# The tower's two state products moved behind the column-tile products, with new places for every step

## What is computed

```python
Z = jnp.einsum('bhsd,bhse->bhsde', v, k)          # k, v after a causal convolution
gl = Z.reshape(Bx, H, Sx, HD * HD) @ gk + gb
gates = (jax.nn.relu(gl) ** 2 + EPS)[..., None]
attn = jnp.cumsum(gates * Z, axis=2) / (jnp.cumsum(gates, axis=2) + EPS)
o = jnp.einsum('bhsd,bhsde->bhse', q, attn)
o = o / jnp.maximum(jnp.linalg.norm(o, axis=3, keepdims=True), EPS)
```

## Time and profile before

| | |
|---|---|
| Median of 3 runs | 1988.42 us (1988.13 to 1988.78) |
| The profiled execution | 1988.27 us, span from first to last instruction 1986.1 us |
| TensorE, TensorE weight loads | busy 1850.2 us (93%), 1588.0 us (80%) |
| VectorE, ScalarE, GpSimd | busy 1165.6 us (59%), 733.4 us (37%), 439.4 us (22%) |
| Granted TensorE clock, mean | 0.982 of full |

### The profile page before, as it was taken

How to read it: one execution, slowest core, us unless ns; L and a number is a source line. 1 busy time by engine, 2 the same in 40 slices (tenths; PEclk the granted TensorE clock), 3 DMA queues, 4 the chain that set the end, 5 groups by cost and what they waited for, 6 DMA issues and landing times.

```text
span 1986.1 us, 41766 instructions
## 1 busy us (share of the span) xinstructions
PE 1850.2 (93%) x17146; PEld 1588.0 (80%) x17146; DVE 1165.6 (59%) x3019; ACT 733.4 (37%) x1444; POOL 439.4 (22%) x391
## 2 busy tenths in 40 slices
PE   4799999999999999969899999999999999999998
PEld 3678888888888888758688888888888888888887
DVE  2668888888888888755554344434444444444443
ACT  1334444554455555334323322232233223322332
POOL 3233223333222222111121122112211221122112
PEclk8899999999999999989899999999999999999999
DMA  3000000000000000022000000000000000000000
GB/s 94 5 12 18 18 17 18 16 19 16 18 17 16 15 5 9 18 86 80 17 22 1 22 22 22 1 22 22 22 1 22 22 22 1 22 22 22 1 22 22
DMA packets 29211, 42.38 MB, mean 21 GB/s; under 512 B 5856, under 2 KB 22624, under 8 KB 29024
## 3 DMA queue, kind: packets, MB, share of 16 engines
q1 hardware_dynamic: 23648, 33.49, 5.1%
q0 software_dynamic: 2048, 4.20, 0.8%
q10 hardware_dynamic: 3328, 2.04, 0.4%
HBM read 22.93 MB, written 16.78 MB: 20 GB/s over the span
## 4 chain that ended last, share of the span: by engine, by line
PE 73%; DVE 17%; issue 4%; DMA 3%; POOL 2%; ACT 1%; SPq 1%; another core or an unknown queue 0%; DVEq 0%; POOLq 0%; ACTq 0%
PE ps L1406 11%; PE ps L1407 10%; PE ps L1408 10%; PE ps L806 3%; PE ps L1008 3%; PE ps L1456 3%; PE ps L1472 3%; DVE bxn L1271 3%; PE ps L887 3%; PE ps L807 3%; PE ps L808 3%; PE ps L959 3%; PE ps L937 2%; DVE bstats L1255 2%; DMA h<-h_rows 2%
## 5 line engine op out<-in xcount | busy, mean ns | idle before, releaser
L1245 POOL TENSOR_TENSOR hids_low<-hid,hids_high 128x512 fp32r<-128x512 f32 x96 | 137.6, 1440 | 611.0 <-ACT hids_high L1392 611.0
L512 POOL TENSOR_TENSOR rstd<-var,minus_half 128x4 f32<-128x4 f32 x80 | 82.5, 1032 | 564.5 <-DVE var L599 564.4
L757 ACT ACTIVATE xn<-x,shift,rstd 128x128 f32<-128x128 f32 x320 | 130.3, 482 | 133.6 <-DVE shift L604 133.6
L676 DVE TENSOR_TENSOR att<-ps,causal 128x512 f32<-128x512 f32 x256 | 158.6, 681 | 18.1 <-PE ps L937 18.0
L1406 PE MATMUL ps<-r_high,wq_high 128*128 128x256 f32 x512 | 147.4, 288 | 0.7 <-issue 0.7
L1407 PE MATMUL ps<-r_low,wq_high 128*128 128x256 f32 x512 | 144.9, 283 | 0.0
L1408 PE MATMUL ps<-r_high,wq_low 128*128 128x256 f32 x512 | 144.8, 283 | 0.0
L1386 ACT ACTIVATE silu<-ps 128x512 f32<-128x512 f32 x96 | 57.4, 598 | 226.5 <-DVE hid L1321 159.9
L1008 PE MATMUL ps<-w_f,wide 128*128 128x128 f32 x1024 | 130.1, 278 | 0.2 <-ACT wide L801 0.2
L1008 PEld LDWEIGHTS ps<-w_f,wide 128*128 128x128 f32 x1024 | 120.8, 192 | 6.0 <-issue 5.0
L1308 DVE TENSOR_TENSOR m_low<-ps,m_high 128x512 fp32r<-128x512 f32 x32 | 22.1, 692 | 170.8 <-ACT m_high L1378 170.8
(11 more groups left out here) (352 smaller groups left out, 5060.9 us busy)
## 6 DMA issues: line engine op xcount, KB each, us to landing
h_rows<-h_out SPq DMA_DIRECT2D x16, 512.0 KB, 2.8
h<-h_rows SPq DMA_DIRECT2D x16, 512.0 KB, 3.8
out<-bxn SPq DMA_DIRECT2D x32, 256.0 KB, 2.6
taps<-in_filters ACTq DMA_DIRECT2D x1, 1024.0 KB
emb<-in_embed,idx POOLq DMA_INDIRECT x64
wk<-in_W_kT SPq DMA_DIRECT2D x1, 1024.0 KB, 6.6
stage<-in_W_vT SPq DMA_DIRECT2D x2, 512.0 KB, 6.6
stage<-in_W_q SPq DMA_DIRECT2D x2, 512.0 KB, 5.6
```

The lines of the kernel that those rows point to most:

```text
L512: pool.tensor_tensor(rstd[s][:], var[s][:], minus_half[:], ALU.pow)\
L676: dve.tensor_tensor(masked[:, :, PAIR * g:PAIR * g + PAIR, :], bank("qk", s, l, j, g, t)[:].rearrange("p (n r t) -> p n r t", n=2, r=PAIR) ...
L757: act.activation(xn[s][:, j, :], x[s][:, j, :], ACT.Identity, bias=shift[s][:, j:j + 1], scale=rstd[s][:, j:j + 1]).then_inc(xn_made[s].se ...
L1245: pool.tensor_tensor(hids[1][:, halves, :], hid[:, half, :], hids[0][:, halves, :].bitcast(F32), ALU.subtract).then_inc(hid_low[s].sem, 1)
```

## The change

**Steps.** The state products leave `av` of tiles 2 and 3. There the first of a tile's products opened the accumulation; now only the first products of tile 0 do (`start=(r == j == 0)`), and all others go without it. A new step `apply` behind the four `av` forms both state products one after the other and adds them onto tiles 2 and 3. `p_av` counts five signals for a layer instead of four: `gk` and the score buffers are freed by the `av` ones as before, `norm` waits for the fifth. The wait for `state_step` moves with the products.

**Places.** All six lists have new numbers. The orders that follow for a steady group, on TensorE: layer 0 was `state, av0, turn, av1, av2, av3` and becomes `state, av0, av1, turn, av2, av3, apply`; layer 1 was `turn, turn, state, av0, av1, turn_v, av2, av3` and becomes `turn, turn, av0, av1, state, av2, av3, turn_v, apply`. `gate` of the next group goes ahead of `unit`, `q` of layer 1 ahead of `turn_v`, `wo` of layer 0 ahead of the convolution of layer 1. After layer 1 the first `head` step goes ahead of `q`. On VectorE: `low` of the final norm goes ahead of `state_low` of layer 1, `f2_out` of layer 0 ahead of `state_low` of layer 0, `wo_out` ahead of the next group's `low`. On ScalarE: the first `conv_out` of layer 0 goes ahead of the last `xn`. On GpSimd: in the layer 0 pass `pow, embed, gather, bias` becomes `pow, bias`; in the layer 1 pass `pow, bias, bias, gather, gather, gather, bias` becomes `pow, bias, embed, bias, bias`. SyncE keeps its order but for the weight loads of the handover. In the second stage the step `t1` of the second sequence goes ahead of both `keys` steps of the first, one `b_gate` ahead of a `b_up`, and VectorE's `b_stats` ahead of `hid`.

```diff
-PLACES_A = [("embed", 0, 0, 750), ("stats", 0, 0, 601), ("pow", 0, 0, 868), ("shift", 0, 0, 710), ("xn", 0, 0, 874),
...
+PLACES_A = [("embed", 0, 0, 479), ("stats", 0, 0, 638), ("pow", 0, 0, 898), ("shift", 0, 0, 713), ("xn", 0, 0, 941),
...
+            ("av", 0, 1, 1662), ("av", 0, 2, 1669), ("av", 0, 3, 1692), ("apply", 0, 0, 1692), ("norm", 0, 0, 1746),
...
+            ("av", 1, 1, 2968), ("av", 1, 2, 2972), ("av", 1, 3, 2975), ("apply", 1, 0, 2983), ("norm", 1, 0, 3313),
...
+    AV = J + 1
...
-    p_av = signals("p_av", J * L)
+    p_av = signals("p_av", AV * L)
...
-            out.append(("gk", ("gk", s, l, t), p_av[s], J * (l + 1)))
+            out.append(("gk", ("gk", s, l, t), p_av[s], AV * l + J))
...
-            out.append(("att", ("att", s, l, j, t), p_av[s], J * l + 2 * j + 2))
+            out.append(("att", ("att", s, l, j, t), p_av[s], AV * l + 2 * j + 2))
...
-            act.wait_ge(p_av[s].sem, p_av[s].at(t, J * (l + 1)))
+            act.wait_ge(p_av[s].sem, p_av[s].at(t, AV * (l + 1)))
...
-            if j == NB:
-                pe.wait_ge(state_step[s].sem, state_step[s].at(t, 3 * l + 3))
             out = bank("av", s, l, t)[:, P * j:P * j + P]
-            if j >= NB:
-                b = j - NB
-                pe.matmul(out, state[s][:, b, :], qT_last[s][:, P * b:P * b + P], start=True, stop=False,
-                          skip_group_check=True)
...
-                                    start=(r == 0 and j < NB), stop=(r == PAIR - 1),
+                                    start=(r == j == 0), stop=(r == PAIR - 1 and j < NB),
                                     skip_group_check=True)
+            ins.then_inc(p_av[s].sem, 1)
+
+        elif step == "apply":
+            pe.wait_ge(state_step[s].sem, state_step[s].at(t, 3 * l + 3))
+            for b in range(NB):
+                ins = pe.matmul(bank("av", s, l, t)[:, P * (NB + b):P * (NB + b) + P], state[s][:, b, :],
+                                qT_last[s][:, P * b:P * b + P], start=False, stop=True, skip_group_check=True)
             ins.then_inc(p_av[s].sem, 1)
```

More of the change, by code:

```diff
@@ L111 @@
[L111 to L117 removed]
+PLACES_A = [("embed", 0, 0, 479), ("stats", 0, 0, 638), ("pow", 0, 0, 898), ("shift", 0, 0, 713), ("xn", 0, 0, 941),
+            ("turn", 0, 0, 890), ("high", 0, 0, 959), ("low", 0, 0, 897), ("bias", 0, 0, 1768), ("q", 0, 0, 981),
+            ("q_out", 0, 0, 1360), ("kv", 0, 0, 922), ("kv_out", 0, 0, 921), ("kv", 0, 1, 924),
+            ("kv_out", 0, 1, 953), ("conv", 0, 0, 947), ("conv_out", 0, 0, 990), ("conv", 0, 1, 952),
+            ("conv_out", 0, 1, 1024), ("turn_v", 0, 0, 976), ("vT_out", 0, 0, 1314), ("gate", 0, 0, 1277),
+            ("gate_mul", 0, 0, 1201), ("gated", 0, 0, 1399), ("state", 0, 0, 1648), ("state_low", 0, 0, 1618),
+            ("qk", 0, 0, 989), ("mask", 0, 0, 985), ("qk", 0, 1, 1567), ("mask", 0, 1, 1472), ("av", 0, 0, 1661),
+            ("av", 0, 1, 1662), ("av", 0, 2, 1669), ("av", 0, 3, 1692), ("apply", 0, 0, 1692), ("norm", 0, 0, 1746),
+            ("sum", 0, 0, 1719), ("chain", 0, 0, 1670), ("unit", 0, 0, 1818), ("unit_out", 0, 0, 1764),
+            ("wo", 0, 0, 1885), ("wo_out", 0, 0, 1895), ("stats", 1, 0, 1897), ("pow", 1, 0, 2336),
+            ("shift", 1, 0, 1958), ("xn", 1, 0, 1991), ("turn", 1, 0, 1963), ("high", 1, 0, 2276),
+            ("low", 1, 0, 1984), ("bias", 1, 0, 2718), ("f1", 0, 0, 1988), ("gelu", 0, 0, 2401), ("f1", 0, 1, 1990),
+            ("gelu", 0, 1, 2407), ("f1", 0, 2, 2187), ("gelu", 0, 2, 2413), ("f1", 0, 3, 2315), ("gelu", 0, 3, 2567),
+            ("f2", 0, 0, 2483), ("f2", 0, 1, 2498), ("f2", 0, 2, 2647), ("f2", 0, 3, 2648), ("f2_out", 0, 0, 2501),
+            ("stats", 2, 0, 2639), ("pow", 2, 0, 2855), ("shift", 2, 0, 2647), ("xn", 2, 0, 2852),
+            ("turn", 2, 0, 2780), ("high", 2, 0, 2882), ("low", 2, 0, 2686), ("bias", 2, 0, 3381), ("q", 1, 0, 2923),
+            ("q_out", 1, 0, 2990), ("kv", 1, 0, 2867), ("kv_out", 1, 0, 2788), ("kv", 1, 1, 2871),
+            ("kv_out", 1, 1, 2815), ("conv", 1, 0, 2894), ("conv_out", 1, 0, 2963), ("conv", 1, 1, 2922),
+            ("conv_out", 1, 1, 2966), ("turn_v", 1, 0, 2924), ("vT_out", 1, 0, 2974), ("gate", 1, 0, 2944),
+            ("gate_mul", 1, 0, 2961), ("gated", 1, 0, 2980), ("state", 1, 0, 2972), ("state_low", 1, 0, 2984),
+            ("qk", 1, 0, 2944), ("mask", 1, 0, 2975), ("qk", 1, 1, 2958), ("mask", 1, 1, 2980), ("av", 1, 0, 2967),
+            ("av", 1, 1, 2968), ("av", 1, 2, 2972), ("av", 1, 3, 2975), ("apply", 1, 0, 2983), ("norm", 1, 0, 3313),
+            ("sum", 1, 0, 2989), ("chain", 1, 0, 2988), ("unit", 1, 0, 3285), ("unit_out", 1, 0, 2991),
+            ("wo", 1, 0, 3471), ("wo_out", 1, 0, 3275), ("stats", 3, 0, 3284), ("pow", 3, 0, 3799),
+            ("shift", 3, 0, 3412), ("xn", 3, 0, 3617), ("turn", 3, 0, 3670), ("high", 3, 0, 3675),
+            ("low", 3, 0, 3635), ("bias", 3, 0, 3856), ("f1", 1, 0, 3701), ("gelu", 1, 0, 3764), ("f1", 1, 1, 3714),
+            ("gelu", 1, 1, 3769), ("f1", 1, 2, 3720), ("gelu", 1, 2, 3863), ("f1", 1, 3, 3810), ("gelu", 1, 3, 3939),
+            ("f2", 1, 0, 3743), ("f2", 1, 1, 3764), ("f2", 1, 2, 3817), ("f2", 1, 3, 3886), ("f2_out", 1, 0, 3866),
+            ("stats", 4, 0, 3871), ("pow", 4, 0, 3998), ("shift", 4, 0, 3921), ("xn", 4, 0, 3998),
+            ("turn", 4, 0, 3964), ("high", 4, 0, 3998), ("low", 4, 0, 3986), ("head", 0, 0, 3987),
+            ("head_out", 0, 0, 3989), ("head", 0, 1, 3998), ("head_out", 0, 1, 3999), ("idx", 0, 0, 782),
+            ("gather", 0, 0, 952), ("gather", 0, 1, 1918), ("gather", 0, 2, 2996), ("gather", 0, 3, 3908),
+            ("store", 0, 0, 3940)]
```

130 lines of the change are left out of this document (49 added, 81 removed).

## The result

The changed kernel takes 1931.83 us (median of 4 runs, 1931.08 to 1932.74) beside 1988.6 for the kernel before: ratio 0.9713, 95% interval 0.9696 to 0.973. Measured again on another chip the ratio was 0.9725 (0.9712 to 0.9738). That is 57 us faster where 38 were forecast, and outside the range. The profiled execution takes 1931.08 us, its span is 1928.9.

A forecast was written before the change was run, and what follows sets the result against it. TensorE was taken to set the tower's pace, its two heavy waits hanging on VectorE's queue. 13 steady groups x (1.8 + 0.9) = 35 us, plus 3 for the other 3 groups, gave 38 us off: 1950, 8-in-10 range 1938 to 1971.

The forecast's parts named there:

- Net nothing, bounds -4 and +4 us: Second stage: the t1 gain of 1.6 us set against start-up and handover, and the chain to xns_low kept.
- the t1 order: Second stage: one t1 step ahead of both keys steps saves a shape change of 64 columns, taken as 0.1 us a group.
- Layer 0: Tower, layer 0 pass: next f1 at 550.25 against 552.08, 1.8 us saved for a steady group.
- The 0.2 us that f1 was to wait for `low`: End of the layer 0 pass: f1 waits some 0.2 us for the `low` that stands behind `state_low`.
- Layer 1: Tower, layer 1 pass: `apply` starts at 530.0, the next step at 530.4; 0.9 us saved (0.2 to 1.5).
- the late `qk`: Layer 1: `q` ahead of turn_v makes q_out late, so `qk` and the masks slip by 0.35 us.
- the middle: Layer 1: start of `apply` taken at 530.0, between 529.3 and 530.7, with TensorE arriving at 529.1.
- Shapes and structure: TensorE: fewer array shape changes and adjacent state products save 0.66 us in layer 0, 0.4 in layer 1, 1.0 a group.
- The GpSimd hold in layer 0: `embed` holds VectorE's L647 and L650; moved elsewhere, they lose 0.62 and 0.47 us and `gk` comes without a wait.
- the cover of `apply`: `state_low` needed after four `av` instead of two: no gain of its own size, since VectorE is late.
- All waits of TensorE vanish: Rival, chance 0.06: 1.8 + 1.5 us for 13 groups and 3 us, 46 us, with the handover's 4: 1938.
- The others: Rivals: GpSimd hold moves and stays, 1968 (0.25); VectorE's run sets the period, 1988 (0.04); late last xn, 2001 (0.04).

The follow-up runs named there:

- high_behind: Kernel before with both second-stage `hid` later on VectorE and the first hids_high behind the next silu on ScalarE; group spacing 0.56 us shorter than before.
- high_between: Changed kernel with the first hids_high of a second-stage group ahead of the fourth silu on ScalarE; 1932.65 us against 1928.84 on the same chip.
- t1_behind: Changed kernel with the second stage's third t1 step back behind the first keys step; ratio 0.9754 to the kernel before.
- changed_again: Changed kernel without any edit, measured once more on another chip; ratio 0.9725, pitch (from one `state` to the next of the same layer) 47.39 us.
- embed_back: Changed kernel with GpSimd's `embed` behind `pow` in the layer 0 pass again; layer 0 pass 1.02 us longer, layer 1 pass unchanged at 10.46.
- embed_early: Kernel before with only GpSimd's `embed` moved ahead of `pow` in the layer 0 pass; tower pitch 0.97 us shorter.
- apply_alone: Kernel before with the new step `apply` right behind the fourth `av` of each layer, every other place kept; tower pitch 0.88 us shorter.
- places_alone: Changed kernel with the state products back in `av`, all other new places kept; 1987.69 us, pitch 51.06 us.
- apply_embed_low: Kernel before with `apply`, `embed` ahead of `pow`, and layer 0's `state_low` behind f2_out; pitch 48.53 us, layer 1 pass 11.54.
- gathers_away: apply_embed_low with two of the three gathers of the layer 1 pass started elsewhere; pitch 49.17 us, layer 1 pass 12.17.
- apply_embed_low_bias: apply_embed_low with GpSimd's bias add ahead of the three gathers instead of behind them; layer 1 pass 11.77 us.
- apply_embed: Kernel before with `apply` behind the fourth `av` and `embed` ahead of `pow` on GpSimd; pitch 48.93 us, 1.99 less.
- hid_ahead: Changed kernel with both second-stage `hid` on VectorE ahead of b_stats and b_xn; ratio 0.0152 above the changed kernel's, 30 us.

## Why the prediction was wrong

**The step that failed** is "Net nothing, bounds -4 and +4 us" for the second stage: it was -12.5. I took the wait on xns_low as the length of its chain of load, statistics and split, wrote that "the new places keep that chain", and didn't look at how long the last link takes and why. In the tower I had looked for the hold by GpSimd; here xns_low, 2.3 us for an operation that takes 1.23 undisturbed, stood in the same trace beside hids_low, and I didn't ask. By the trace, a group changed by -1.04 (the wait before the gram), -0.10 (first to second gram), +0.58 (the new wait on gram_low) and -0.22 (from t1 to r, where I took -0.1): -0.78 in all, -0.80 in the spacing. That the hold makes and takes away the wait is shown from both sides by high_behind and high_between, the price of the t1 order by t1_behind. My term stood at nothing; with -12.5 in its place, and all else as I had it, the sum gives 1937.5.

**Mis-sized terms in the tower.** 44.8 us instead of 38.
- Layer 0: 2.04 to 2.07 against 1.8. `state` starts 13.20 us behind `sum` (519.36 less 506.16; I had 13.2), so that part was right. The 0.2 us that f1 was to wait for `low` did not come.
- Layer 1: 1.77 on the pass against 0.9. What lies outside the two passes grew by 0.77 us a group (50.92 - 19.28 - 12.23 against 47.85 - 17.21 - 10.46), by 0.33 in changed_again; L938 on qT_last and L900 on kc wait there. I had set 0.35 for the late `qk`, inside the 0.9. I took `apply` at 0.9 behind TensorE's arrival, "the middle"; it starts on arrival, 10.09 us behind the first qk, and my parts add up to 10.05. VectorE's run had become shorter by the floor step's hold (1.16 to 0.57) and by that of L641 (0.53 to 0.19, L642 in the changed kernel), which I did not list at all. The floor step's hold no longer sets the pass there: in embed_back it is gone (0.19 us) and the pass is 10.46 still.
- 13 x 3.07 = 39.9; the start and the handover to the second stage gave 4.9 more where I had 3.

**Right.** Shapes and structure: in layer 1 the parts add up to 10.05 for 10.09. The GpSimd hold in layer 0, its two lines and its price, shown by embed_early and embed_back. That it would go and not move holds for the whole new order, not for the place of `embed` by itself, since in embed_early a part of it falls on the floor step of layer 1. That the cover of `apply` would not show as a gain by itself, shown by apply_alone; I did not see that places_alone would give nothing either. f2_out ahead of `state_low` is no loss but a gain of 0.4.

**The rivals.** "All waits of TensorE vanish" comes close to what the tower did, and its 46 us, without the 4 for the handover, would have been near the 44.8; I gave it 0.06. Its 1938 has nothing for the second stage either. The others fell: nothing waits for the last xn from one group to the next.

**Shown and open.** For layer 0 all parts are shown one by one. In layer 1 the 1.08 us between apply_embed_low and the changed kernel are shown in part: with the lost time of TensorE and the hold of the floor step both away, gathers_away comes to 10.89 by the sum above, which is 0.65 of them, and the other 0.43 rest on the changed kernel's trace alone. The holds move on in apply_embed_low_bias and gathers_away, and no run but the changed kernel has them all off the layer 1 pass. Also open: what the gathers have to do with the gaps, and why turn_v waits for kc in one execution and not in another.

## What to carry to other kernels

In a trace with GpSimd at work, list every VectorE operation on the path with its minimum and its median, in all stages; where they differ, or where the price is out of line with its size, ask which of the two engines starts first and what sets that, since a place on a third engine can turn it. A wait is to be read together with the duration of what it waits for. Two edits that each remove one of two waits in series are worth little alone: price them together, and don't take the middle where TensorE's own time already is a lower bound and the rest hangs on holds that can be listed.

## What the runs showed of the hardware

- Behind gathers started by GpSimd TensorE can stand still for 0.4 to 0.8 us inside the gate and column-tile matmuls, ending 0.7 or 1.7 us behind the start of the last gather (six times in apply_embed_low, six in apply_alone, twice in the kernel before). Where it lies inside an `av`, VectorE stands still up to the same moment, to 0.03 us. It went when the gathers were moved, and is missing in apply_embed and embed_early, where they were not. The profile names no releaser, and no run tells by what way a gather could reach the two engines.
- The hold between VectorE and GpSimd goes by who starts first, down to 0.07 us, and its price was 1.07 us on xns_low, 1.83 on `gk` where a gather and a bias add follow each other, and 0.6 to 1.2 on 128x32 steps that take 0.18 or 0.19 alone.
- In hid_ahead a wait of 2.1 us is followed by 5 us at a mean granted clock of 0.79, and the stage costs 2.0 us a group; the changed kernel's longest waits there are 0.9 us.
